# An attention and feed-forward kernel: part of VectorE's attention work moved to GpSimd, and VectorE's slot reordered

## What is computed

```python
x = x + layernorm(attention(layernorm(x)))
x = x + layernorm(ffn(layernorm(x)))
# attention, 16 heads of 64, keys and values from one matrix w_kv
q = l2norm(heads(x @ w_q)) * exp(scale);  k = l2norm(heads(x @ w_k));  v = heads(x @ w_v)
out = softmax(q @ k.T) @ v;  return merge(out) @ w_out + b_out
# ffn, 256 -> 1024 -> 1024 -> 1024 -> 256, ternary weights with one scale per output
h = silu((x @ w1.T) * w1_s) * ((x @ w2.T) * w2_s)
h = gelu((h @ h1.T) * h1_s);  h = gelu((h @ h2.T) * h2_s);  return (h @ w3.T) * w3_s
```

## Time and profile before

| | us |
|---|---|
| median of 3 runs | 1945.36 |
| lowest and highest run | 1936.95, 1945.42 |
| the profiled execution, its own time | 1939.09 |
| its span, first to last instruction | 1937.2 |
| busy in it: TensorE, VectorE, ScalarE, GpSimd | 1743.2, 1203.1, 1012.1, 426.7 |

### The profile page before, as it was taken

One profiled execution on the slowest core, in us unless ns is written; L12 is line 12 of the kernel. 1 busy time (PEld: TensorE's weight loads), 2 busy tenths in 40 slices (PEclk: granted clock), 3 DMA queues, 4 the chain that ended last, 5 costly groups with the idle time before them and its releaser, 6 DMA issues.

```text
span 1937.2 us, 24570 instructions
## 1 busy us (share of the span) xinstructions
PE 1743.2 (90%) x8584; PEld 1443.8 (75%) x8584; DVE 1203.1 (62%) x2085; ACT 1012.1 (52%) x1349; POOL 426.7 (22%) x499
## 2 busy tenths in 40 slices
PE   4899899999899889989988984699999999999997
PEld 3677777778678778777777773587878778777876
DVE  4676786786686776776776765664443544444453
ACT  2776676777677667767766763213232331313231
POOL 3333423423323423333333320000000000000000
PEclk8999999999999999999999997799999999999999
DMA  3534544535435445455344355310000000000000
GB/s 117 120 83 116 120 98 115 115 98 121 110 100 121 109 106 132 107 116 129 87 115 111 80 137 132 112 60 2 23 2 23 14 13 23 2 23 2 24 2 22
DMA packets 71445, 152.03 MB, mean 78 GB/s; under 512 B 25968, under 2 KB 26224, under 8 KB 71280
## 3 DMA queue, kind: packets, MB, share of 16 engines
q1 hardware_dynamic: 63504, 122.34, 27.0%
q10 hardware_dynamic: 6624, 23.21, 3.8%
q0 software_dynamic: 1152, 4.19, 0.5%
HBM read 56.91 MB, written 20.19 MB: 40 GB/s over the span
## 4 chain that ended last, share of the span: by engine, by line
PE 51%; DMA 22%; DVE 12%; issue 7%; SPq 4%; ACT 2%; POOL 1%; DVEq 0%; ACTq 0%; POOLq 0%
DMA work<-rows 13%; PE pair L1087 12%; PE pair L1088 12%; PE bank L1009 6%; DMA Dp<-work 5%; PE bank L1023 4%; PE bank L951 4%; DMA rows<-Rp 3%; DVE Pl L675 3%; PE pair L1078 3%; PE pair L1079 2%; DVE work L691 2%; SPq L252 2%; SPq L251 2%; PE bank L1116 2%
## 5 line engine op out<-in xcount | busy, mean ns | idle before, releaser
L1009 PE MATMUL bank<-Ph,V 128*128 128x512 f32 x1024 | 379.9, 412 | 103.3 <-DVE Pl L675 102.9
L1087 PE MATMUL pair<-hh,f 128*128 128x512 f32 x1024 | 405.6, 396 | 18.1 <-DVE hl L787 9.9
L468 ACT ACTIVATE P<-pair,sh 128x1024 f32<-128x1024 f32 x256 | 286.4, 1119 | 246.3 <-PE pair L993 135.6
L1088 PE MATMUL pair<-hl,f 128*128 128x512 f32 x1024 | 404.1, 395 | 0.0
L1009 PEld LDWEIGHTS bank<-Ph,V 128*128 128x128 f32 x1024 | 198.7, 194 | 176.8 <-issue 131.6
L675 DVE TENSOR_TENSOR Pl<-P,Ph 128x1024 fp32r<-128x1024 f32 x256 | 311.9, 1218 | 1.0
L513 ACT ACTIVATE hr<-pair,ct 128x512 f32<-128x512 f32 x128 | 88.2, 689 | 378.8 <-PE pair L1088 378.8
L473 ACT ACTIVATE Ph<-P 128x1024 fp32r<-128x1024 f32 x256 | 271.6, 1061 | 8.1
L1087 PEld LDWEIGHTS pair<-hh,f 128*128 128x128 f32 x1024 | 195.7, 191 | 63.3 <-issue 12.8
L1088 PEld LDWEIGHTS pair<-hl,f 128*128 128x128 f32 x1024 | 195.7, 191 | 41.3 <-issue 0.6
L358 POOL TENSOR_TENSOR rs<-ss,half 128x8 f32<-128x8 f32 x128 | 214.3, 1674 | 10.7
(11 more groups left out here) (101 smaller groups left out, 2852.2 us busy)
## 6 DMA issues: line engine op xcount, KB each, us to landing
stack<-turned SPq DMA_DIRECT2D x128, 384.0 KB, 4.5
stack<-turned SPq DMA_DIRECT2D x128, 256.0 KB, 5.1
work<-rows SPq DMA_DIRECT2D x64, 256.0 KB
f<-raw ACTq DMA_DIRECT2D x22, 512.0 KB, 4.9
raw<-in_h ACTq DMA_DIRECT2D x16, 512.0 KB, 5.3
xt<-in_x SPq DMA_DIRECT2D x8, 512.0 KB, 8.6
xr<-in_x SPq DMA_DIRECT2D x8, 512.0 KB, 8.8
x<-xr SPq DMA_DIRECT2D x8, 512.0 KB, 3.0
```

What stands on the lines that cost most here:

```text
L468: e.activation(M.P[:, i % 2, :], M.SB[i % 2][:, :], ACT.Exp, bias=M.sh[:, h:h + 1]).then_inc(S["exp"])
L1009: d = e.matmul(M.OB[:, :], v, p[:, u % 3, j * 512:(j + 1) * 512], start=jt == 0 and m == 0, stop=jt == 3 and m == 2)
L1087: e.matmul(ps, w, M.hh[src][:, k, :].bitcast(to), start=k == 0, stop=False)
L1088: d = e.matmul(ps, w, M.hl[src][:, k, :].bitcast(to), start=False, stop=k == KH - 1)
```

## The change

Of each pair's multiply by reciprocals, the even head's instruction moves to GpSimd (`normal_even`) and the odd head's stays on VectorE (`normal_odd`), both in slot 4n + 10, one slot later than `normal` was. GpSimd makes the high and the low half of the pair right behind its part, ahead of `head_root` of the same slot. `ln1b` and `finish2` move to GpSimd. On VectorE, `head_scale` comes ahead of `head_sums`, `v_low` and `turn_low`, and `ln1` and `finish` are placed in other slots and ahead of them too. `x_turn` moves one slot forward, `x_low` one slot back, and `x_high` of the first half to the head of ScalarE's slot 21. The bank plan gives x a longer hold. The diff, with the engines' unchanged functions left out:

```diff
@@ bank_plan, L101: x_turn of the next batch in slots 19 and 20 of a batch, not 20 and 21
-        if b + 1 < B and i % 32 in (20, 21):
+        if b + 1 < B and i % 32 in (19, 20):
...
-        last[bank], free[bank] = user, i + n / len(order) + (user[0] == "qk")
+        last[bank], free[bank] = user, i + n / len(order) + {"qk": 1, "x": 1.5}.get(user[0], 0)
@@ free3 L170, spread_rec L269, evacuate L477: two counters for one
-    q.wait_ge("on", 2 * NP)
+    q.wait_ge("ona", NP)
+    q.wait_ge("onb", NP)
...
@@ pool_program
+    def normal_even(n):
+        q.wait_ge("nl", n - 1)
+        q.wait_ge(f"rb{n % 2}", 16 * (n // 2 + 1))
+        q.wait_ge("ev", 2 * n + 1)
+        e.tensor_tensor(M.on[0:64, n % 2, :], M.Ev[0:64, (2 * n) % 4, :], M.Rb[0:64, n % 2, :],
+                        ALU.mult).then_inc(S["onb"])
...
     def o_high(n):
-        q.wait_ge("on", 2 * n + 2)
+        q.wait_ge("ona", n + 1)
+        q.wait_ge("onb", n + 1)
...
+    def o_low(n):
+        q.wait_ge("nh", n + 1)
+        e.tensor_tensor(M.nl[:, n % 2, :], M.on[:, n % 2, :], M.nh[:, n % 2, :].bitcast(f32),
+                        ALU.subtract).then_inc(S["nl"])
...
     norm_root(0)
+    for t in range(NT):
+        ln1b(0, t)
...
     for i in range(SLOTS):
...
+        if i % 4 == 2 and 0 <= i // 4 - 2 < NP:
+            normal_even(i // 4 - 2)
+            o_high(i // 4 - 2)
+            o_low(i // 4 - 2)
         for u in tiles_of(i):
             head_root(u)
-        if i % 4 == 1 and 0 <= i // 4 - 2 < NP:
-            o_high(i // 4 - 2)
         if i - NU == 8:
             out_root(B - 1)
-        if 0 <= pb < B - 1 and i32_ == 9:
-            out_root(pb)
-        if b + 1 < B and i32_ == 13:
-            norm_root(b + 1)
+        if i - NU == 9:
+            for t in range(NT):
+                finish2(B - 1, t)
+        if 0 <= pb < B - 1:
+            if i32_ == 11:
+                out_root(pb)
+            if i32_ in (12, 13):
+                finish2(pb, 2 * (i32_ - 12))
+                finish2(pb, 2 * (i32_ - 12) + 1)
+        if b + 1 < B:
+            if i32_ == 7:
+                norm_root(b + 1)
+            if i32_ == 15:
+                for t in range(NT):
+                    ln1b(b + 1, t)
@@ act_program: x_high(b + 1, 0) ahead of exp(i) in slot 21, x_high(b + 1, 1) where it was
@@ vector_program: ln1b, finish2 and o_low are gone, normal(n) is now
+    def normal_odd(n):
+        q.wait_ge("nl", n - 1)
+        q.wait_ge(f"rb{n % 2}", 16 * (n // 2 + 1))
+        q.wait_ge("ev", 2 * n + 2)
+        e.tensor_tensor(M.on[64:128, n % 2, :], M.Ev[64:128, (2 * n + 1) % 4, :], M.Rb[64:128, n % 2, :],
+                        ALU.mult).then_inc(S["ona"])
...
     for i in range(SLOTS):
...
-        if i % 4 == 2 and 0 <= n - 3 < NP:
-            o_low(n - 3)
         if i % 4 == 3 and 0 <= n - 2 < NP:
             invert(n - 2)
+        if i % 4 == 2 and 0 <= n - 3 < NP:
+            normal_odd(n - 3)
+        if b + 1 < B and i32_ in (21, 22):
+            x_low(b + 1, i32_ - 21)
+        if tail == 8:
+            for t in range(NT):
+                finish(B - 1, t)
+        if 0 <= pb < B - 1:
+            for t in {8: (0,), 9: (1, 2), 11: (3,)}.get(i32_, ()):
+                finish(pb, t)
+        if b + 1 < B:
+            for t in {3: (0,), 4: (1, 2), 6: (3,)}.get(i32_, ()):
+                ln1(b + 1, t)
+        for u in tiles_of(i - 1) if i else []:
+            head_scale(u)
         for u in tiles_of(i):
             head_sums(u)
...
-        for u in tiles_of(i - 1) if i else []:
-            head_scale(u)
-        if i % 4 == 1 and 0 <= n - 3 < NP:
-            normal(n - 3)
```

More of the change, by code:

```diff
@@ L100, in bank_plan @@
             order += [(("y", 2 * quad_of(i)), i), (("y", 2 * quad_of(i) + 1), i)]
-        if b + 1 < B and i % 32 in (20, 21):
-            order.append((("x", 2 * (b + 1) + i % 32 - 20), i))
+        if b + 1 < B and i % 32 in (19, 20):
+            order.append((("x", 2 * (b + 1) + i % 32 - 19), i))
         if i == NU - 3:
@@ L268, in spread_rec @@
         q.wait_ge(f"rw{n % 2}", 16 * (n // 2 + 1))
-        q.wait_ge("on", 2 * (n - 1))
+        q.wait_ge("ona", n - 1)
+        q.wait_ge("onb", n - 1)
         row = M.rows[n].rearrange("(o a) b -> o (a b)", o=2).unsqueeze(1).to_broadcast([2, 64, 512])
@@ L361, in head_root, with ln1b, finish2 @@
         e.tensor_tensor(rs, rs, M.eq[:, qd, :, :, :].rearrange("p b c d -> p (b c d)"), ALU.mult).then_inc(S["rq"])
+    def normal_even(n):
[4 more added lines that the diff above has]
+                        ALU.mult).then_inc(S["onb"])
     def o_high(n):
-        q.wait_ge("on", 2 * n + 2)
+        q.wait_ge("ona", n + 1)
+        q.wait_ge("onb", n + 1)
         q.wait_ge("out", 2 * (n // 2) - 2)
         e.tensor_copy(M.nh[:, n % 2, :], M.on[:, n % 2, :]).then_inc(S["nh"])
+    def o_low(n):
+        q.wait_ge("nh", n + 1)
+        e.tensor_tensor(M.nl[:, n % 2, :], M.on[:, n % 2, :], M.nh[:, n % 2, :].bitcast(f32),
+                        ALU.subtract).then_inc(S["nl"])
+    def ln1b(b, t):
+        q.wait_ge("rd", b + 1)
+        e.tensor_scalar(M.xt[:, t, :], M.xt[:, t, :], M.mv[:, t, 0:1], M.rd[:, t:t + 1],
+                        ALU.subtract, ALU.mult).then_inc(S["xn"])
+    def finish2(b, t):
+        q.wait_ge("rd2", b + 1)
+        e.tensor_scalar(M.y[:, t, :], M.y[:, t, :], M.mv2[:, t, 0:1], M.rd2[:, t:t + 1],
+                        ALU.subtract, ALU.mult).then_inc(S["yn"])
+        q.wait_ge("yn", NT * b + t + 1)
+        q.wait_ge("xr", 16 * (b + 1))
+        e.tensor_tensor(M.xr[:, t, :], M.xr[:, t, :], M.y[:, t, :], ALU.add).then_inc(S["x1r"])
     def out_root(b):
@@ L476, in evacuate @@
         q.wait_ge("pv", 2 * g + 2)
-        q.wait_ge("on", 2 * (g // 2 - 1))
+        q.wait_ge("ona", g // 2 - 1)
+        q.wait_ge("onb", g // 2 - 1)
         q.wait_ge("wl", WPOS[6])
@@ L537, in act_program @@
         g, c, b, r, live = slot(i)
+        if b + 1 < B and i % 32 == 21:
+            x_high(b + 1, 0)
         if live:
@@ L553, in act_program @@
             turn_high(pair_of(i), 0)
-        if b + 1 < B and i % 32 in (20, 21):
-            x_high(b + 1, i % 32 - 20)
+        if b + 1 < B and i % 32 == 21:
+            x_high(b + 1, 1)
         if HEAD <= i < HEAD + 7:
@@ L618, in ln1 @@
             e.tensor_scalar_add(M.ve[:, :], M.mv[:, :, 1], EPS).then_inc(S["ve"])
[L620 to L623, removed]
     def x_low(b, k):
@@ L683, in invert @@
         e.reciprocal(M.Rp[:, n % 2, :], M.Dp[:, n % 2, :]).then_inc(S["rp"])
-    def normal(n):
+    def normal_odd(n):
         q.wait_ge("nl", n - 1)
[L687 to L698, removed]
+        q.wait_ge(f"rb{n % 2}", 16 * (n // 2 + 1))
+        q.wait_ge("ev", 2 * n + 2)
+        e.tensor_tensor(M.on[64:128, n % 2, :], M.Ev[64:128, (2 * n + 1) % 4, :], M.Rb[64:128, n % 2, :],
+                        ALU.mult).then_inc(S["ona"])
     def add_part(Q, half):
@@ L717, in finish @@
             e.tensor_scalar_add(M.ve2[:, :], M.mv2[:, :, 1], EPS).then_inc(S["ve2"])
[L719 to L725, removed]
     def count_piece(n):
@@ L810, in vector_program @@
         ln1(0, t)
-    for t in range(NT):
-        ln1b(0, t)
     x_low(0, 0)
@@ L857, in vector_program @@
             add_part(quad_of(i), 1)
[L858 to L876, removed]
         if HEAD <= i < HEAD + 7:
@@ L1155, in tensor_program @@
             outp(quad_of(i), 1)
-        if b + 1 < B and i % 32 in (20, 21):
-            x_turn(b + 1, i % 32 - 20)
+        if b + 1 < B and i % 32 in (19, 20):
+            x_turn(b + 1, i % 32 - 19)
         if i == NU - 3:
```

## The result

**The change made the kernel slower: 1997.1 us (median of 4 runs, 1993.91 to 2001.17) against 1945.39 us, a ratio of 1.0276 [1.0242, 1.0311].** The forecast was 1920 us, with a range from 1893 to 1950. The profiled execution's span is 1992.1 us, 54.9 more than before. The timelines of ScalarE split it by the first and the last exponential: 22.0 us lie before the first one (68.6 against 46.6 us), 30.0 in the attention, 2.9 behind it. Batches 1 to 6 last 149.3 us each, where they lasted 144.2.

A forecast was written before the change was run, and what follows sets the result against it. TensorE bounds the kernel, waiting on a VectorE late, not full. Slot 3 -4.6, clock -7, batch 0 -6.7, end -3, start +0.5 make -20.8: span 1916.4, plus 1.9 and 2, forecast 1920 us, range 1893 to 1950.

The forecast's parts named there:

- item 3: Even pairs: slots 3, 11, 19 stop waiting; tile 3's root behind GpSimd's pieces brings 1.0 us waits in slots 5, 13, 21, 29.
- Item 5: Next batch's x: xl comes 0.6 us later, and slots 20 to 22 wait 3.3 us instead of 1.69.
- the clock: Steady stretch: of some 20 us lost to the clock, a third hangs on slot 15's 2 us waits: -7 us.
- The first reading: TensorE is the bound and waits 78.2 us for VectorE's Pl and xl; VectorE is late, not full.
- any case of mine: The four forecast times for the whole kernel: 1920, 1898, 1961 and 1937 us.
- item 1: VectorE gives work away: worth nothing by itself, counting only where Pl stood behind normal's 1.4 us.
- Items 2 and 4: GpSimd's load, odd pairs and outp: finish2 and ln1b pieces cost 0; outp nets 0; slot 15's wait falls 2.08 to 0.7.
- Half these prices: GpSimd's finish2 and ln1b pieces of 256 columns priced at half the 1.2 us of a 512-column piece.
- The two-input price: GpSimd's half multiply and residual: 1.2 us each, twice the 0.61 us cast; a skill-based estimate gave 1.1 us.
- rival C: Roots behind residuals on GpSimd: each 0.1 us more costs 0.2 us a block, gain gone at 1.57; 1961 us, chance 0.14.
- The start: Ahead of slot 0: four ln1b on GpSimd lie on the path, +0.5 us (-0.3 to +1.5).
- Clock and end: Steady stretch and from 1100 us on: clock -7 us, granted clock above 0.98; end -3 us (-6 to +3).

The follow-up runs named there:

- order_x_old: order_alone with x_turn, x_high, x_low and the bank plan as in the kernel before; 1885.41 us, ratio 0.9678.
- order_alone: residual_back with the half multiply on VectorE too: nothing moved to GpSimd, the change's order kept; 1910.06 us, ratio 0.9821.
- residual_back: norms_back with the residual on VectorE, ahead of Pl in slots 3 mod 4; 1934.76 us, ratio 0.9954.
- norms_back: start_fixed with finish2 and ln1b on VectorE again; 1948.44 us, ratio 0.9999.
- start_fixed: The changed kernel with x's longer bank hold only from batch 1 on; 1979.33 us, ratio 1.0168.
- split_norms: norms_back with even pairs' cast and residual behind tile 3's root in GpSimd's queue; 1925.60 us, ratio 0.9919.
- bank_alone: The kernel before with only x's longer hold of 1.5 in the bank plan; 1956.96 us, ratio 1.0066.
- move_mended: split_norms with x_turn, x_high, x_low and the bank plan as in the kernel before; 1913.80 us, ratio 0.9841.
- order_x_cast: order_x_old with even pairs' cast behind tile 3's root on GpSimd, not ahead of it; 1981.72 us, ratio 1.0193.

## Why the prediction was wrong

By the ladder of ratios, from the order alone to the change: .9678 (order_x_old), then the change's x path (`x_turn`, `x_high`, `x_low` and the bank plan) +28 us (order_alone, .9821), half multiply +26 (residual_back, .9954), residual +9 (norms_back, .9999), norms +33 (start_fixed, 1.0168), bank hold +21 (the change, 1.0276). By the intervals each step is known to some 8 to 16 us only, and each is the price of a piece beside the others that were there: the x path costs 12 to 15 us, not 28, beside the split.

The forecast was 25 us under the time before, the measurement 52 over it. Of these 77 us the norms and the bank hold make 54, and the prediction had both at next to nothing. With both out (norms_back) the kernel is as fast as before, where 25 us were to be won; that is left for items 3, 5 and the clock.

**The first reading was right.** VectorE was late, not full. Taking `normal` from ahead of Pl and letting each slot's work follow its readiness won 3.2%, more than any case of mine gave. But the order does that; no work had to leave VectorE. I had this in item 1 ("worth nothing by itself") and never took the next step: to ask what the order gives without the move. Between the first and the last exponential order_x_old's profile is 52.0 us shorter than the one before: 33.1 of it is idle time of TensorE (107.7 and 74.6), and 19 are matmuls that ran faster, at a granted clock of 0.980 against 0.968. The order is a bundle, though: the multiply a slot later, the residual ahead of Pl, the cast ahead of the root, `head_scale` and the norms in other places. No run takes it apart.

**Item 3 failed by its size.** The mechanism was the one I wrote down: waits in slots 5, 13 and 29 and, through the bank instead of Pl, in 20; those of 3, 11 and 19 went. But it is 2.1 to 2.3 us and not 1.0. The chain that I priced at 4.2 us (multiply, cast, residual) took 1.29 + 1.55 + 1.29 and its gaps, 4.3, in the timeline of slots 89 to 93, GpSimd first, then VectorE, and TensorE's wait that follows:

```profile
485.13 1.15 POOL L357 TENSOR_SCALAR ss<-ss 128x8 f32<-128x8 f32 x1 [2.28 <-DVE ss L687]
486.37 2.06 POOL L360 TENSOR_TENSOR rs<-ss,half 128x8 f32<-128x8 f32 x1
488.50 0.20 POOL L363 TENSOR_TENSOR rs<-rs,eq 128x8 f32<-128x8 f32 x1
488.66 1.29 POOL L370 TENSOR_TENSOR work<-work 64x512 f32<-64x512 f32 x1
490.08 1.55 POOL L377 CAST nh<-work 128x512 fp32r<-128x512 f32 x1
491.70 1.29 POOL L381 TENSOR_TENSOR nl<-work,nh 128x512 fp32r<-128x512 f32 x1
492.97 0.24 POOL L357 TENSOR_SCALAR ss<-ss 128x8 f32<-128x8 f32 x1
...
484.96 1.22 DVE L717 TENSOR_TENSOR Pl<-P,Ph 128x1024 fp32r<-128x1024 f32 x1
486.21 0.69 DVE L732 TENSOR_TENSOR work<-work 64x512 f32<-64x512 f32 x1
488.74 0.69 DVE L696 TENSOR_TENSOR qk<-bank,rs 128x512 f32<-128x512 f32 x1 [1.84 <-POOL rs L363]
...
495.27 0.69 DVE L696 TENSOR_TENSOR qk<-bank,rs 128x512 f32<-128x512 f32 x1 [4.00 <-POOL rs L363]
...
497.90 0.47 PE L1024 MATMUL bank<-Ph,V 128*128 128x512 f32 x1 [2.08 <-DVE Pl L717]
```

What I missed stands at the head of it: I let tile 2's root take 2.35 us, as in the earlier trace rows, though I had moved Pl to right behind the sums that start it. Beside Pl the root's first piece took 1.15 us instead of 0.24, and beside the odd half its second took 2.06 instead of 1.67. The root, ready to start at 485.1, ends at 488.70, 3.6 us later, and all behind it comes 1.2 us late. 1.0 + 1.2 is about the wait that came. split_norms shows the link to the chain: with cast and residual behind the root, slots 13 and 29 wait 0.62 and slot 20 not at all. That the hold of the root alone makes the 1.2 is read from durations and was not tried by itself.

**Items 2 and 4 costed the norms at zero, which is the step that failed by the most: 33 us.** "Half these prices" was a wrong scale. A TENSOR_SCALAR of 256 columns took 1.32 and 1.64 us in the mean, no less than a half multiply of 512 columns that isn't held up by VectorE (1.29), against 0.49 on VectorE. And "GpSimd at 35% busy" is no cover for a block: what counted was that 10.8 us in one piece stood ahead of a chain that `outp` needs. Slot 15, which I let fall from 2.08 to 0.7, has 3.07 in the mean (2.48 before), and 0.82 with the norms back.

**The two-input price was nearly right,** 1.29 us by the median and 1.36 in the mean, for 1.2. The estimate of 1.1 us that I worked out from the Trainium skill's GPSIMD Engine Reference (Elementwise — side-by-side cycle accounting) is lower than the 1.26 us of the shortest. A good price did not help: rival C had the right mechanism, yet its tipping price of 1.57 was never reached. Its price of 0.2 us per 0.1 us left out the root's own hold and the norms.

**The start, costed at +0.5, was +22.0.** The bank plan is part of the change, and I followed only its later batches. bank_alone shows 18.7 of it, and start_fixed takes 19.0 back.

**Item 5** had the direction: slots 20 and 22 wait 4.4 us, where I said 3.3. That this part of the change costs 12 to 28 us, by what stands beside it (move_mended, order_x_old), I did not see, since I wrote it down as 1.6 us a batch against the earlier trace rows and left out the clock.

**Clock and end** gave nothing back: 0.97 for the "above 0.98" I wanted, and 2.9 us more behind the last exponential for 3 less. It wasn't a loss either: over the attention the granted clock is 0.966 against 0.968.

**The half multiply** costs 26 us on GpSimd, and the prediction, which walked it in item 3, has no term of that size. Between the first and the last exponential the profiles of residual_back and order_alone differ by 23.6 us (1159.9 and 1136.3). TensorE's idle time makes 13 of them (106.2 and 93.2); in the rest the same matmuls ran slower, at a granted clock of 0.963 against 0.970. `outp` waits 34.0 us for the residual in the steady stretch, where order_alone has 24.5. The other part is new and lies in slots 12 and 28, 0.5 and 0.6 us each, as in order_x_cast: the residual stands ahead of Pl and waits for a cast that now follows GpSimd's half. The rows of residual_back, 100 to 1100 us:

```profile
DVE nl L713 <- POOL nh L377: 20.5, 32, 1.2
PE bank L1025 <- issue: 10.2, 20, 0.7
```

In order_alone the first of these waits comes once in the whole kernel, for 0.7 us, and the second is 1.4 us. So part of the price belongs to the residual's place, which no run varied; why the clock fell with it stays open.

## What to carry to other kernels

When a queue is late and not full, try the new order by itself before moving work to another engine: here the order won some 60 us and the move, in the best place tried, gave 28 back. Before placing work on an idle engine, look for what stands behind it in that engine's queue and who waits for that, and count the block's whole length, not the engine's mean load. A planner's constant changed for one user is read again for every user that its test lets in, those at the start of the program first.

## What was not expected of the hardware

A TENSOR_SCALAR with two operands per partition takes GpSimd 1.22 us for 128x256, by the median (1.23 in finish2), twice the 0.61 of a 128x512 cast. A TENSOR_TENSOR of 512 columns takes 1.29 us, on 64 partitions as on 128.

VectorE and GpSimd hold each other up, both ways. The Trainium skill (SBUF — State Buffer, Who interferes with whom) calls the port pair that the two share an exclusive lock. The trace agrees on GpSimd's side, where an operation on 8 columns went from 0.24 to 1.15 us beside a Pl of 1.22. On VectorE's side Pl's mean rose from 1218 ns in the kernel before to 1270 in the changed one (the group above), and to 1303 in split_norms:

```profile
L702 DVE TENSOR_TENSOR Pl<-P,Ph 128x1024 fp32r<-128x1024 f32 x256 | 333.6, 1303 | 0.0
```

An instruction that is held up need not cost much, though. In order_x_old, the fastest kernel, the root's second piece takes 2053 ns in the mean, against 1674 in the kernel before:

```profile
L360 POOL TENSOR_TENSOR rs<-ss,half 128x8 f32<-128x8 f32 x128 | 262.8, 2053 | 10.7
```
